# A two-layer graph network on one core: two bias rows added by POOL, a check squared on ACT, lists in another order

## What is computed

```python
def layer0(src, adj):                      # 8 heads of 32
    q, k = src @ Wq + bq, src @ Wk + bk
    attn = softmax(q @ k.T / sqrt(32))
    out = sum((attn * (adj == r)) @ (src @ Wv[r] + bv[r]) for r in range(4))
    x = ln(src + out @ Wo + bo, g1, beta1)
    return ln(x + gelu(x @ W1 + b1) @ W2 + b2, g2, beta2)

def layer1(f, adj):
    e = leaky_relu((f @ Lq) @ (f @ Lk).T, 0.2)
    h = softmax(where(adj > 0, e, -9e15)) @ (f @ Lv)
    return ln(concat(ln(h), f) @ Wffn.T) + f
```

## Time and profile before

| | |
|---|---|
| median of 3 runs | 3328.57 us (3326.73 to 3330.99) |
| the profiled execution | 3329.45 us, its span 3327.6 us |
| PE busy | 3141.7 us, 94% |
| weight loads (PEld) busy | 2713.8 us, 82% |
| DVE busy | 2795.0 us, 84% |
| ACT busy | 2098.1 us, 63% |
| POOL busy | 1474.6 us, 44% |
| DMA | 292.63 MB, 34% of 16 engines |
| granted TensorE clock, mean | 0.991 |
| chain that ended last | PE 62%, SP queue 10%, DVE 7%, POOL 7%, DMA 6%, ACT 4%, issue 4% |

### The profile page before, as it was taken

How to read it: one execution, slowest core, us unless ns; L and a number is a source line. 1 busy time by engine, 2 the same in 40 slices (tenths; PEclk the granted TensorE clock), 3 DMA queues, 4 the chain that set the end, 5 groups by cost and what they waited for, 6 DMA issues and landing times.

```text
span 3327.6 us, 77390 instructions
## 1 busy us (share of the span) xinstructions
PE 3141.7 (94%) x28930; PEld 2713.8 (82%) x28930; DVE 2795.0 (84%) x4892; ACT 2098.1 (63%) x4300; POOL 1474.6 (44%) x1549
## 2 busy tenths in 40 slices
PE   3899999999999999999999999999999999999996
PEld 2788888888888888888888888888888888888885
DVE  3688888888888888888888888888888888888885
ACT  2466666666666666666666666666666666666664
POOL 1345345344444444444444444444444444444441
PEclk8999999999999999999999999999999999999998
DMA  3333333333433433423433433433433433433331
GB/s 105 81 89 82 101 81 86 102 79 85 105 76 86 107 76 86 107 76 86 107 76 86 107 76 86 107 76 86 107 76 86 107 76 86 106 77 86 104 74 33
DMA packets 217643, 292.63 MB, mean 88 GB/s; under 512 B 31492, under 2 KB 119048, under 8 KB 217608
## 3 DMA queue, kind: packets, MB, share of 16 engines
q1 hardware_dynamic: 217608, 292.16, 34.2%
HBM read 72.89 MB, written 16.78 MB: 27 GB/s over the span
## 4 chain that ended last, share of the span: by engine, by line
PE 62%; SPq 10%; DVE 7%; POOL 7%; DMA 6%; ACT 4%; issue 4%; POOLq 0%; DVEq 0%; ACTq 0%
PE pair L920 32%; PE pair L950 11%; SPq L309 8%; DMA stack_a<-qk 5%; PE pair L974 5%; POOL probs L408 4%; PE pair L1033 3%; PE pair L965 3%; DVE n L686 3%; PE pair L966 3%; ACT probs L529 2%; POOL rstd L398 2%; PE pair L925 2%; DVE qk L738 2%; ACT qk L516 2%
## 5 line engine op out<-in xcount | busy, mean ns | idle before, releaser
L402 POOL TENSOR_TENSOR act_r_lo<-act,act_r_hi 128x512 fp32r<-128x512 f32 x256 | 345.7, 1356 | 654.0 <-DVE act_r_hi L765 523.0
L502 ACT ACTIVATE leaky_s<-pair 128x1024 f32<-128x1024 f32 x256 | 260.5, 1029 | 436.6 <-PE pair L966 436.6
L508 ACT ACTIVATE leaky_s<-leaky_s,low_r 128x256 f32<-128x256 f32 x1024 | 506.6, 496 | 10.9 <-DVE low_r L728 4.1
L732 DVE TENSOR_REDUCE mx_a<-pair 128x4 f32<-128x1024 f32 x256 | 306.4, 1217 | 114.0 <-PE pair L1033 113.9
L408 POOL TENSOR_TENSOR probs<-probs,rel 128x512 f32<-128x512 f32 x256 | 309.6, 1229 | 164.2 <-ACT probs L529 164.2
L396 POOL TENSOR_TENSOR rstd<-mv,eps 128x2 f32<-128x2 f32 x256 | 72.6, 284 | 660.0 <-DVE mv L675 660.0
L529 ACT ACTIVATE probs<-pair 128x1024 f32<-128x1024 f32 x256 | 263.1, 1029 | 127.8 <-PE pair L1042 125.4
L498 ACT ACTIVATE probs<-pair 128x1024 f32<-128x1024 f32 x256 | 260.5, 1019 | 86.2 <-PE pair L974 81.9
L724 DVE TENSOR_TENSOR leaky_s<-pair,leaky_s 128x1024 f32<-128x1024 f32 x256 | 306.7, 1219 | 5.2 <-ACT leaky_s L502 5.2
L728 DVE TENSOR_REDUCE low_r<-leaky_s 128x4 f32<-128x1024 f32 x256 | 304.0, 1208 | 0.0
L408 POOL TENSOR_TENSOR leaky_s<-probs,rel 128x512 f32<-128x512 f32 x256 | 300.7, 1204 | 0.0
(11 more groups left out here) (180 smaller groups left out, 9112.3 us busy)
## 6 DMA issues: line engine op xcount, KB each, us to landing
stack_a<-qk SPq DMA_DIRECT2D x768, 128.0 KB, 2.9
stack_r<-qk SPq DMA_DIRECT2D x768, 128.0 KB, 2.4
xt<-in_xT SPq DMA_DIRECT2D x64, 256.0 KB, 3.2
adj_a<-in_adjT SPq DMA_DIRECT2D x64, 256.0 KB, 3.1
xn<-in_x SPq DMA_DIRECT2D x64, 256.0 KB, 3.0
adj_q<-in_adj SPq DMA_DIRECT2D x64, 256.0 KB, 3.0
out<-n SPq DMA_DIRECT2D x64, 256.0 KB, 2.2
probs<-in_w SPq DMA_DIRECT2D x4, 512.0 KB, 5.1
```

The lines of the kernel that those rows point to most:

```text
L402: return nc.gpsimd.tensor_tensor(dst, src, hi, ALU.subtract)
L508: last = nc.scalar.activation(leaky_s[:, p % SLOTS, k, t], leaky_s[:, p % SLOTS, k, t], ACT.Exp, bias=low_r[:, p, k, t:t + 1], accum_out=d ...
L732: return nc.vector.tensor_reduce(mx_a[:, :, p * NG:(p + 1) * NG].rearrange("p t h -> p h t"), pair[b][:], AX.X, ALU.max)
```

## The change

It takes the four bias products of out_projection and of the last down chunk from PE. The rows bo and b2 are loaded into norm (broadcast over partitions) and added by POOL with a new function: xn + bo in place when xn has landed, and x1 + b2 into xn later. DVE's two residual adds read xn both times and wait for POOL (xn_bo; for the second add only down_part, and the order of POOL's list, stand in between). The check becomes (adj - 0.5) squared with a sum over the row, on ACT; it is 0.25 an entry for 0 and 1 alike, and DVE keeps the maximum. Third, all lists, the PSUM banks and the waits that go with them are written in another order; vee(1) and wk change places, out_projection comes after vee(0), one(1) and masked_rows(2) move to the following turn, row_products lv moves there too, and SP issues each turn's twelve DMAs for stack_r and twelve for stack_a without a load in between.

```diff
-        bias_r = sb("bias_r", [SHIFT, 4 * D], F32R)
-        bv_r, bo_r, b2_r = bias_r[:, 0:2 * D], bias_r[:, 2 * D:3 * D], bias_r[:, 3 * D:]
-        norm = sb("norm", [P, 8, D])
+        bias_r = sb("bias_r", [SHIFT, 2 * D], F32R)
+        bv_r = bias_r[:]
+        norm = sb("norm", [P, 10, D])
...
-        B_AO, B_ADEN, B_Q, B_K, B_WO, B_X1T, B_RV, B_HN = 2, 4, 3, 7, 4, 6, 3, 4
-        B_DN, B_N1T, B_FFN, B_AMT, B_X2T, B_LQ, B_LK, B_LV = 3, 3, 0, 7, 5, 3, 6, 1
+        B_AO, B_ADEN, B_Q, B_K, B_WO, B_X1T, B_RV, B_HN = 4, 5, 5, 1, 3, 3, 1, 1
+        B_DN, B_N1T, B_FFN, B_AMT, B_X2T, B_LQ, B_LK, B_LV = 6, 3, 0, 4, 1, 1, 6, 2
...
+            def with_row(dst, src, r):
+
+                for t in range(NT):
+                    last = nc.gpsimd.tensor_tensor(dst[:, t], src[:, t], norm[:, r], ALU.add)
+                return last
...
                 if g1 is not None:
+                    pool.wait_ge(ld_xn.sem, ld_xn.at(g1))
+                    with_row(xn, xn, BO).then_inc(xn_bo.sem, 1)
                     pool.wait_ge(ln_mv[LN_A].sem, ln_mv[LN_A].at(g1))
                     make_rstd(LN_A, g1)
...
                     low(act_lo[:, 2], act[:, 2], act_hi[:, 2]).then_inc(act_split.sem, 1)
+                    with_row(xn, x1, B2).then_inc(x1_b2.sem, 1)
                     pool.wait_ge(act_hi_done.sem, act_hi_done.at(g1))
...
+                if g2 is not None and not path.general:
+                    act_e.wait_ge(rel1_done.sem, rel1_done.at(g2))
+                    nc.scalar.activation(adj_a[:].bitcast(F32), adj_a[:], ACT.Square, bias=half[:], accum_out=known[:]
+                                         ).then_inc(known_done.sem, 1)
...
-                if g2 is not None and not path.general:
-                    nc.vector.scalar_tensor_tensor(adj_a[:], adj_a[:], 0, rel1[:], ALU.is_equal, ALU.add,
-                                                   accum_out=known[:]).then_inc(known_done.sem, 1)
...
-                    nc.vector.tensor_tensor(res[:], bank(B_DN), x1[:], ALU.add).then_inc(res_m_done.sem, 1)
+                    nc.vector.tensor_tensor(res[:], bank(B_DN), xn[:], ALU.add).then_inc(res_m_done.sem, 1)
...
+                    dve.wait_ge(xn_bo.sem, xn_bo.at(g2))
                     nc.vector.tensor_tensor(res[:], bank(B_WO), xn[:], ALU.add).then_inc(res_a_done.sem, 1)
...
-                    products(bank(b)[:, t], lambda i, g: parts[i][:, g, t * P:(t + 1) * P], whole(W["wo"]), NG, stop=False)
-                    last = add_bias(bank(b)[:, t], bo_r)
+                    last = products(bank(b)[:, t], lambda i, g: parts[i][:, g, t * P:(t + 1) * P], whole(W["wo"]), NG)
...
-                if c == NCH - 1:
-                    for t in range(NT):
-                        last = add_bias(bank(B_DN)[:, t], b2_r, skip=True)
-                    last.then_inc(down_mm.sem, 1)
```

More of the change, by code:

```diff
@@ L345, in body @@
                     stack(1, stack_r, stacked_r)
+                    stack(3, stack_r, stacked_r)
                     stack(2, stack_r, stacked_r)
                 if g3 is not None:
[L348 to L352, removed]
+                    sp.wait_ge(qk_split.sem, qk_split.at(g3))
+                    stack(1, stack_a, stacked_a)
+                    stack(3, stack_a, stacked_a)
+                    stack(0, stack_a, stacked_a)
+                    stack(2, stack_a, stacked_a)
                 if g0 is not None:
@@ L356, in body @@
                 if g3 is not None:
[L357 to L361, removed]
+                    load(adj_a, adjT, g3, "(t p) n -> p t n", ld_adj_a)
+                if g2 is not None:
+                    load(adj_q, adj, g2, "(t p) n -> p t n", ld_adj_r)
             turns(sp, body)
@@ L548, in body @@
                     copy(v_a[:, 0], bank(B_V[0])).then_inc(v_done.sem, 1)
+                    act_e.wait_ge(q_mm.sem, q_mm.at(g2))
+                    biased(1, B_K, bk_c).then_inc(qk_hi_done.sem, 1)
                     act_e.wait_ge(v_mm.sem, v_mm.at(g2))
                     copy(v_a[:, 1], bank(B_V[1])).then_inc(v_done.sem, 1)
-                    act_e.wait_ge(q_mm.sem, q_mm.at(g2))
-                    biased(1, B_K, bk_c).then_inc(qk_hi_done.sem, 1)
+                if g0 is not None:
+                    act_e.wait_ge(turned_mm.sem, turned_mm.at(g0, 1))
+                    copy(probs[:, :, 0], pair[B_TN[0]][:]).then_inc(probs_r.sem, 1)
+                    act_e.wait_ge(sr_mm.sem, sr_mm.at(g0, 3))
+                    low(2, B_RR[2]).then_inc(low_done.sem, 1)
                 if g1 is not None:
@@ L556, in body @@
                 if g0 is not None:
-                    act_e.wait_ge(turned_mm.sem, turned_mm.at(g0, 1))
-                    copy(probs[:, :, 0], pair[B_TN[0]][:]).then_inc(probs_r.sem, 1)
+                    act_e.wait_ge(low_r_done.sem, low_r_done.at(g0, 2))
+                    exp_rows(1).then_inc(exp_r_done.sem, 1)
                     act_e.wait_ge(sr_mm.sem, sr_mm.at(g0))
@@ L577, in body @@
                     exp_rows(3).then_inc(exp_r_done.sem, 1)
-                    act_e.wait_ge(turned_mm.sem, turned_mm.at(g0, 2))
-                    copy(probs[:, :, 1], pair[B_TN[1]][:]).then_inc(probs_r.sem, 1)
                     act_e.wait_ge(turned_mm.sem, turned_mm.at(g0, 3))
@@ L858, in body @@
                     centre(LN_O, bank(B_FFN), LG2, result)
+                if g1 is not None:
+                    dve.wait_ge(low_done.sem, low_done.at(g1, 1))
+                    leaky(0, B_RR[0]).then_inc(leaky_done.sem, 1)
                 if g2 is not None:
@@ new lines, in body @@
+                if g3 is not None:
+                    dve.wait_ge(sa_mm.sem, sa_mm.at(g3, 1))
+                    maximum(0, B_AR[0]).then_inc(mx_a_done.sem, 1)
+                if g2 is not None:
+                    dve.wait_ge(act_done.sem, act_done.at(g2))
+                    dve.wait_ge(down_part.sem, down_part.at(g2, 1))
+                    nc.vector.tensor_copy(act_hi[:, 0], act[:, 0]).then_inc(act_hi_done.sem, 1)
+                if g3 is not None:
+                    dve.wait_ge(sa_mm.sem, sa_mm.at(g3, 2))
+                    maximum(1, B_AR[1]).then_inc(mx_a_done.sem, 1)
```

322 lines of the change are left out of this document (157 added, 165 removed).

## The result

The changed kernel takes 3376.9 us (median of 4 runs, 3374.7 to 3378.9) where the kernel before took 3328.1 in the same series: ratio 1.0145, 95% interval 1.0128 to 1.0163. It is slower by 49 us. The prediction was 3269, with a range of 3215 to 3334. The time after lies outside it, on the other side.

A forecast was written before the change was run, and what follows sets the result against it. PE was taken as the bound; its saved work and waits, less a new wait, took a turn from 50.07 to 49.10 us, -59 us over 61 full turns, giving 3269 us, range 3215 to 3334.

The forecast's parts named there:

- The bias products: Four products of 256 columns leave PE each turn; all their time counts: -0.47 us a turn.
- POOL's adds: Four new adds a turn, 2.9 us on POOL, priced at 0; first pair at most 1.5 us a turn.
- Rival C: Slower: POOL's new adds hold up DVE or delay its add of xn; 3343, or 3404 with both pairs; chance 0.17.
- The check: Moved from DVE to ACT's idle time before the copy of att: 0, bounds 0 and -0.7 us a turn.
- The waits that go: PE's waits at first and third score_rows, att's transposes and both(0) vanish, -1.29; up(0)'s shrinks from 0.68 to 0.3, -0.38.
- The transposes of n1: DVE's rescales still end 7.96 us after the first score_cols starts; PE waits 0.28 instead of 0.38: -0.10 us.
- The new wait: PE waits for stack_r's copies before the second masked_rows: +1.27 us a turn, bounds 0.9 and 2.4.
- PE's own work: 47.7 us of the 50.07 us turn, changed only by the bias products taken away.
- my walk: New lists timed with old row durations from the first score_cols' start, putting the second masked_rows at 15.08 us.
- The signs that I had named as right: 49.1 us turn, no 256-column L925, PE waiting over 1 us for stack_r, hardly for stack_a, n1's transposes waiting for DVE.
- those named as wrong: Turn under 48.3; turn of 50 with PE waiting at score_rows; long DVE rows beside POOL's adds or xn's add waiting.

The follow-up runs named there:

- e5: e4 with the four bias products a turn back on PE and POOL's four adds removed: 3334.2 us, ratio 1.0030 to the kernel before.
- e11: Kernel before with 64 bytes of unused tile, so later tiles lie as in e8, nothing else changed: 3337.2 us, ratio 1.0025.
- e8: Kernel before with only the check moved to an ACT Square, its two extra tiles shifting later tiles 64 bytes: 3336.7 us, ratio 1.0039.
- e3: Changed kernel with POOL's second masks waiting for the end of DVE's rescales of n: 3320.3 us, ratio 0.9987 to the kernel before.
- e1: Changed kernel plus one unused 4-byte tile behind half, making the later tiles' shift 64 bytes: 3356.2 us, ratio 1.0106 to the kernel before.
- e4: e1 with POOL's second masks waiting for the end of DVE's rescales of n: 3299.5 us, ratio 0.9922 to the kernel before.
- e7: e1 with DVE's cast of xt_hi moved behind the two splits of query and key: 3299.9 us, ratio 0.9925 to the kernel before.
- e12: Changed kernel, no pad, with its new tile half allocated behind all other tiles: 3347.5 us, ratio 1.0056 to the kernel before.
- e2: Kernel before plus one unused 4-byte tile that shifts later tiles by 32 bytes: 3357.2 us, ratio 1.0097.

## Why the prediction was wrong

- **The bias products, -0.47.** Right, 0.10 too small: 0.57 a turn with POOL's adds in it (e5).
- **POOL's adds, 0.** Right (e5). Rival C named the right mechanism at the wrong place. DVE is held up by POOL, but by its old masks, not by the new adds. That C's prices, 3343 and 3404, lie on either side of 3377 is luck.
- **The check, 0.** Right, once e11 took the tiles' places out of e8.
- **The waits that go, -1.29 and -0.38.** Right as far as waits go: none of note is left at those places. At up(0) more went than the 0.38: of 0.68 us 0.15 are left.
- **The transposes of n1, "This chain is unchanged".** This is the step that failed. The list of DVE around the chain is unchanged, but what feeds it isn't. I moved x2's transposes behind two more score_cols on PE, took the 0.35 us that this gives to both(0), and did not carry the delay on to ACT's copy and DVE's x2t_lo, which stand ahead of the cast. DVE came 0.44 us later, and what had been 0.20 us ahead of POOL's masks was now 0.22 behind. That made 0.44 into 1.39. The trace had the warning: the rescales of 2.49 us beside POOL's masks stood in the earlier trace rows, and I used it for the new adds only. It came to 0.97 to 0.99 us a turn (after less e3, e1 less e4, e1 less e7), 59 us by 61 turns, more than the whole loss of 49.
- **The new wait, +1.27.** Right in place and, from SP's start to the second masked_rows, in length: 5.85 us against 5.77. Its price, by starts as in my walk, was 1.25 in e4, where the late chain is out of the way: 0.32 ahead of the first group (it starts 1.32 us after the values products ahead of it began, in the changed kernel, where it does not wait, 1.00) and 0.93 ahead of the second. one(1) put back between won the 0.93.
- **PE's own work, taken as unchanged.** The second step that failed. `half` moved the tiles, and the same products came later one after another: 0.46 us a turn, 30 us (e12). The rows before had products of 256 columns at 0.11 as well as at 0.12 us, and I did not ask what sets which; that a tile's place does, nothing there told. No term or bound of the sum could hold it, and the range was too narrow for it.

The two together are 0.97 + 0.46 = 1.43 of the 1.72 us by which the turn was off. The remaining 0.29 lies ahead of the copies. In e4, where nothing makes n1's transposes wait, they start straight behind lk at s + 8.03; my walk had lk end at s + 7.75. Four score_cols with two transposes took 3.21 us (1605.91 to 1609.12), where I had 3.05, and both, lq and lk 4.82, where I had 4.70. So SP begins at s + 9.58 (9.60 in e3) and not at 9.31. Without the late chain (e3) and with the tiles back (0.46), a turn would be 49.39 if the two add up, which was not run, against my 49.10.

The signs that I had named as right did hold for the L925 rows, for stack_a and for n1's transposes; the wait for stack_r was at its place, but of 0.73 us a turn and not over 1. Of those named as wrong none fitted. A turn over 50 without a wait at score_rows and without long rows beside POOL's adds was not on my list.

## What to carry to other kernels

Before calling a chain unchanged, carry the new start of each operand through all engines that feed it, and compare it with what runs beside it: where DVE and POOL pass each other within a few tenths of a us, a small delay can be multiplied (0.44 to 1.39 here). Such a race is better settled by a wait or by moving the short instruction out of the way (e3, e7) than left to luck. A new small tile belongs behind all others, and an experiment that adds one needs a control with the tile alone; without e11 the Square would have been blamed for 12 us.

## What the runs showed of the hardware

- POOL's mask products on 128x512 stretch some of DVE's instructions beside them and not others. The cast of 128x512 took 0.42 us alone and 1.02 (e7) or 1.40 (after) caught, two rescales of 128x256 0.88 alone and 2.49 to 2.68 beside. DVE's split from PSUM took 0.68 beside masks (L820 after) and 0.69 with no POOL instruction beside it (L680 after, xt_r_lo). The Trainium skill, "SBUF — State Buffer", section "SBUF: two separate sides", has DVE and GpSimd sharing a port pair that one of them holds for a whole instruction; the 0.98 us added to the cast agrees with it, and is less than one mask product (1.25 us).
- The time of unchanged PE work depends on where the tiles lie in a partition. 32 bytes more cost the kernel before 0.97% (0.80 to 1.14), 64 bytes 0.25% (0.14 to 0.35), with the granted clock at 0.99 throughout. The pace of the products by w2 was 118.2 and 118.5 ns with the two shifts against 113.5, so that pace alone does not rank the kernels. What differs is a wait: between 1000 and 2000 us PE waited for stack_a 6.6 us before, 7.2 in e2 and 2.3 in e11, so in e11 the slower products mostly fill a wait. Why the copies come in time there was not followed. Which tile matters, and how its address acts, stays open; it was not tried.
